# Two of sixteen row maxima as 512-element passes beside a positive difference on ScalarE, and the maxima turned by VectorE instead of TensorE

## What is computed

```python
y = einsum('bsi,oi->bso', x, sign(weight / s)) * (s * scale_param)   # s: mean |weight| of a row
scores = einsum('bhqd,bhkd->bhqk', q, k) / sqrt(16)
attn = softmax(scores, axis=-1)
out = einsum('bhqk,bhkd->bhqd', attn, v)
...
hidden = silu(x @ gate_w.T) * (x @ up_w.T)
x = x + attention(xn) + hidden @ down_w.T
```

## Time and profile before

| | |
|---|---|
| median of 3 runs | 503.11 us (502.55 to 505.74) |
| profiled execution | 502.01 us, of which the span is 500.3 us |
| PE busy | 482.1 us |
| DVE busy | 416.9 us |
| ACT busy | 348.3 us |
| POOL busy | 94.6 us |
| mean granted PE clock | 0.996 |

### The profile page before, as it was taken

How to read it: one execution, slowest core, us unless ns; L and a number is a source line. 1 busy time by engine, 2 the same in 40 slices (tenths; PEclk the granted TensorE clock), 3 DMA queues, 4 the chain that set the end, 5 groups by cost and what they waited for, 6 DMA issues and landing times.

```text
span 500.3 us, 10322 instructions
## 1 busy us (share of the span) xinstructions
PE 482.1 (96%) x4186; PEld 163.9 (33%) x4186; DVE 416.9 (83%) x487; ACT 348.3 (70%) x655; POOL 94.6 (19%) x138
## 2 busy tenths in 40 slices
PE   1899999999998999999999999999999999999996
PEld 1564444433332222222222222222222233333442
DVE  7879869676777999999999999999999955224986
ACT  1943643352338999999999999999999978874000
POOL 4212244434323000000000000000000113241021
PEclk9999999999998999999999999999999999999999
DMA  8843673732103702102102211211120124452321
GB/s 269 273 95 98 163 151 42 200 74 25 20 1 54 135 24 64 41 24 64 41 24 65 41 36 50 42 57 29 42 63 24 35 78 112 105 148 80 104 84 43
DMA packets 31302, 39.02 MB, mean 78 GB/s; under 512 B 6608, under 2 KB 20816, under 8 KB 31256
## 3 DMA queue, kind: packets, MB, share of 16 engines
q1 hardware_dynamic: 22232, 27.34, 18.9%
q0 software_dynamic: 8304, 10.95, 11.9%
q10 hardware_dynamic: 720, 0.08, 0.1%
HBM read 33.24 MB, written 10.35 MB: 87 GB/s over the span
## 4 chain that ended last, share of the span: by engine, by line
PE 94%; DVE 3%; ACT 1%; DMA 1%; issue 1%; ACTq 0%; SPq 0%; DVEq 0%
PE ps L1319 28%; PE ps L1135 19%; PE ps L1250 15%; PE ps L1144 10%; PE ps L1211 5%; PE ps L1198 5%; PE ps L1114 4%; PE ps L1353 3%; PE ps L1286 2%; DVE stats L768 1%; ACT room L709 1%; DVE room L790 1%; PE ps L1106 1%; PE ps L1155 1%; DMA hlo<-x 1%
## 5 line engine op out<-in xcount | busy, mean ns | idle before, releaser
L842 DVE TENSOR_REDUCE nmx<-ps 128x1 f32<-128x1024 f32 x248 | 284.1, 1216 | 14.2 <-PE ps L1144 13.9
L709 ACT ACTIVATE room<-ps 128x512 f32<-128x512 f32 x512 | 271.5, 602 | 21.5 <-PE ps L1286 11.0
L1319 PE MATMUL ps<-room,vcur 128*32 128x256 f32 (+1 forms) x1880 | 159.6, 411 | 0.7 <-ACT room L709 0.7
L1144 PE MATMUL ps<-kA,qst 48*128 48x512 f16 x496 | 142.4, 384 | 0.0
L1250 PE MATMUL ps<-qst,kB 50*128 50x512 f16 x432 | 135.6, 385 | 0.6 <-DVE room L941 0.4
L1135 PE MATMUL ps<-room,wf 128*128 128x512 f16 x448 | 100.6, 379 | 0.0
L1319 PEld LDWEIGHTS ps<-room,vcur 128*32 128x32 f32 x1880 | 37.2, 108 | 94.6 <-issue 53.9
L689 ACT ACTIVATE room<-ps,gsc 128x512 f32<-128x512 f32 x28 | 19.3, 688 | 61.8 <-PE ps L1135 61.8
L1135 PEld LDWEIGHTS ps<-room,wf 128*128 128x128 f16 x448 | 42.4, 98 | 55.1 <-issue 7.2
L1250 PEld LDWEIGHTS ps<-qst,kB 50*128 50x128 f16 x432 | 27.7, 93 | 92.6 <-ACT room L709 71.9
L546 POOL TENSOR_TENSOR hlo<-room,hhi 128x512 f16<-128x512 f32 x28 | 34.0, 1216 | 87.2 <-ACT hhi L619 87.2
(11 more groups left out here) (136 smaller groups left out, 319.4 us busy)
## 6 DMA issues: line engine op xcount, KB each, us to landing
qst<-q_scratch SPq DMA_DIRECT2D x32, 192.0 KB, 3.6
o_scratch<-osb SPq DMA_DIRECT2D x16, 256.0 KB, 2.3
q_scratch<-parts SPq DMA_DIRECT2D x12, 256.0 KB
hlo<-x SPq DMA_DIRECT2D x8, 256.0 KB, 4.6
parts<-x POOLq DMA_DIRECT2D x8, 256.0 KB, 3.9
wf<-gate POOLq DMA_DIRECT2D x14, 128.0 KB, 3.8
wf<-up POOLq DMA_DIRECT2D x14, 128.0 KB, 5.9
wd<-down POOLq DMA_DIRECT2D x1, 1792.0 KB, 13.5
```

Of the source, the lines that this page charges most:

```text
L709: nc.scalar.activation(probs[:, s % 2, r, :], ps[:, bank_of(gp, s, i), :], ACT.Exp, scale=gam_reg[par][r]).then_inc(scores_free, 1)
L842: nc.vector.tensor_reduce(nmx[:, hf, idx:idx + 1], bank_pair(idx % 2), AX.X, ALU.max, negate=True).then_inc(rows_free, 1)
L1144: return nc.tensor.matmul(ps[:, 2 * (idx % 2) + b, :], qst[low:low + KROWS, par, hf, head, qt * P:(qt + 1) * P], kA[low:low + KROWS, par, ...
L1319: mm = nc.tensor.matmul(ps[32 * r:32 * r + 32, values_bank(step_ // TT), of], vcur[:, par, key_tile(r, j), :], probs[:, s % 2, r, of], sta ...
```

## The change

**Two units of sixteen take another form.** In the steps with `step % 8` 4 and 6 before `LATE` (`PAIRED`, `paired`; 26 steps in all) the first of the step's two units is a pair. Its PE matmul on bank 0 uses, instead of the keys of the first half, half the *difference* of the keys of the two halves (`kD`), so that bank 0 holds half of a - b, where a and b are the scores of a query with key n and key n + 512; bank 1 holds b as before. ACT computes `excess` = Relu(2 x bank 0) into SBUF, between its first and second exponential of that step. DVE then makes one pass over 512 elements, bank 1 plus `excess` (that is max(a, b)), with the minimum of the negated sum as its result (`row_max_paired`). The pass waits for ACT's `excess_ready`. The number of PE's matmuls stays.

**The differences.** POOL forms them once from the projected keys in four 128x512 operations (`difference`), among its feed-forward work; SP stores them to `d_scratch` and loads 48 x 512 of them for each group. The evacuation of the values projection on DVE waits for the first of the four.

**The turn of the maxima.** POOL now scales and splits the 128 x 16 table itself, in three 128x16 operations (`split_max`), DVE transposes it in blocks of 32 x 32 (`turn_max`, one 128x32 instruction between the two units of a block's second step), and SP stores it with eight transfers of 2 x 16 x 32 elements instead of four of 16 x 128. PE's transpose, its bank of the ring, and ACT's `take_max` are gone.

```diff
+    PAIRED = [4, 6]
+
+    def paired(step):
+        return step < LATE and step % TT in PAIRED
...
-        if j == T_STEP:
-            taken.append(("t", block_ + 1))
-        elif j == T_STEP + 1:
-            freed.append(("t", block_ + 1))
...
+            def load_differences(g, par):
+                sp.dma_start(kD[0:KROWS, par, :],
+                             d_scratch[bass.ds(g, 1)].rearrange("g t d n -> (g t d) n")).then_inc(kD_loaded[par], 16)
+
             def load_shift(v, par, hf):
                 sp.wait_ge(shift_ready, v + 1)
-                for low in (0, HI):
-                    for part in range(2):
-                        row = low + KROWS + part
-                        dst = qst[row:row + 1, par, hf].rearrange("p h n -> p (h n)")
-                        sp.dma_start(dst, shp[:, hf, part, :]).then_inc(shift_loaded[par][hf], 16)
+                for row in (KROWS, HI + KROWS):
+                    dst = qst[row:row + 2, par, hf].rearrange("p h (t b n) -> p (h t) b n", b=P // SQ, n=SQ)
+                    for b in range(P // SQ):
+                        sp.dma_start(dst[:, :, b, :], shp[b * SQ:(b + 1) * SQ, hf, :]).then_inc(shift_loaded[par][hf], 16)
...
             def split_max(v, hf):
 
-                pool.wait_ge(max_taken, v + 1)
-                nc.gpsimd.tensor_tensor(shp[:, hf, 0, :], mxs[:, :], ones[0:UNITS, :], ALU.mult).then_inc(shift_step, 1)
-                pool.wait_ge(shift_step, v + 1)
-                nc.gpsimd.tensor_tensor(shp[:, hf, 1, :], mxs[:, :], shp[:, hf, 0, :], ALU.subtract).then_inc(shift_ready, 1)
-
+                pool.wait_ge(rows_free, 2 + (v + 1) * UNITS)
+                pool.wait_ge(shift_ready, v)
+                nc.gpsimd.tensor_tensor(mxs[:, :], nmx[:, hf, :], unlift[:, :], ALU.mult).then_inc(split_step, 1)
+                nc.gpsimd.tensor_tensor(mxp[:, 0:UNITS], nmx[:, hf, :], unlift[:, :], ALU.mult).then_inc(split_step, 1)
+                pool.wait_ge(split_step, 2 * (v + 1))
+                nc.gpsimd.tensor_tensor(mxp[:, UNITS:2 * UNITS], mxs[:, :], mxp[:, 0:UNITS],
+                                        ALU.subtract).then_inc(split_ready, 1)
+
+            def difference(stage):
+
+                if stage == 0:
+                    pool.wait_ge(sign_ready, 3)
+                    pool.wait_ge(guarded, 2)
+                    nc.gpsimd.tensor_tensor(diff, y[:, 0, 0:HALF], y[:, 0, HALF:T], ALU.subtract).then_inc(diff_step, 1)
+                elif stage == 1:
+                    pool.wait_ge(diff_step, 1)
+                    pool.wait_ge(out_factors_ready, 1)
+                    nc.gpsimd.tensor_scalar(diff, diff, k_down[:, 0:1], 0.5, ALU.mult, ALU.mult).then_inc(diff_step, 1)
+                elif stage == 2:
+                    pool.wait_ge(diff_step, 2)
+                    nc.gpsimd.tensor_copy(diff_parts[:, 0, :], diff).then_inc(diff_step, 1)
+                else:
+                    pool.wait_ge(diff_step, 3)
+                    nc.gpsimd.tensor_tensor(diff_parts[:, 1, :], diff, diff_parts[:, 0, :],
+                                            ALU.subtract).then_inc(diff_ready, 1)
...
-                if j == t_step(step // TT) + 1 and not (last and s >= STEPS + TT):
-                    block_ = gp * 4 + s // TT
-                    take_max(block_ + 1, LATE_T if step >= LATE else ring_bank["t", block_ + 1])
                 act.wait_ge(probs_free, step + 1)
...
+                    if i == 0 and paired(step):
+                        act.wait_ge(excess_due, pairs_before(step) + 1)
+                        before = [p for p in range(step) if paired(p)]
+                        if before:
+                            act.wait_ge(rows_free, 2 + 2 * UNITS + 2 * before[-1] + 1)
+                        nc.scalar.activation(excess, ps[:, 0, :], ACT.Relu, scale=2.0).then_inc(excess_ready, 1)
...
+            def turn_max(v, hf):
+
+                dve.wait_ge(split_ready, v + 1)
+                nc.vector.transpose(shp[:, hf, :], mxp[:, :]).then_inc(shift_ready, 1)
+
+            def row_max_paired(n, hf, idx, pairs):
+
+                dve.wait_ge(rows_ready, n + 1)
+                dve.wait_ge(excess_ready, pairs + 1)
+                nc.vector.tensor_tensor_reduce(gr[:, 0:HALF], ps[:, 1, :], excess, -1.0, TOP, ALU.add, ALU.min,
+                                               nmx[:, hf, idx:idx + 1]).then_inc(rows_free, 1)
...
-                        mm = half_rows(1 - par, hf, idx, 1 - half)
+                        if i == 0 and paired(step):
+                            assert half == 1
+                            pe.wait_ge(kD_loaded[1 - par], 16 * ((gp_ * 2 + par + 2) // 2))
+                            mm = half_rows(1 - par, hf, idx, 0, kD)
+                            mm.then_inc(excess_due, 1)
+                        else:
+                            mm = half_rows(1 - par, hf, idx, 1 - half)
...
-                if j == T_STEP:
-                    ring_free(("t", block_ + 1))
-                    transpose_max(block_ + 1, 1 - hf, ring_bank["t", block_ + 1])
```

99 lines of the change are left out of this document (57 added, 42 removed), and 2 rows, old and new, of the table dve_order.

## The result

The changed kernel takes 511.63 us (median of 6 runs, 510.25 to 514.26), the kernel before in the same runs 502.89: a ratio of 1.0169, 95% interval 1.0133 to 1.0205. It is slower by 8.7 us, inside the range of 502 to 514, and 3.5 us above the forecast. The profiled execution of it took 512.35 us, with a span of 510.6.

The account below looks back on a forecast made before the run. PE was taken to bound the attention loop, with DVE 0.1 us from it; +5.7 us in the loop, -0.3 for the half block and -0.4 outside gave +5.0 on 503.1, 508.1 us, range 502 to 514.

Parts of the forecast that it names:

- TensorE's floor of 1.11 and 17.76 a block: Attention loop: PE's half step never takes less than 1.11 us, so a block's sixteen halves take 17.76.
- relief rival: Attention loop: PE runs at its floor, 17.91 us a block, 0.30 less than before; 498.7 us in all; chance 0.12.
- Taking the transpose off PE alone would bring nothing: Attention loop: without the pairs, a block would still end at DVE's 18.10 us plus the new turn.
- The fourth exponential's delay, 0.33 a paired step: Paired steps: ACT's fifth operation makes PE's values matmuls start 0.33 us later, 0.66 a block.
- The whole block, 18.65: Attention loop: 17.76 + 0.09 + 0.06 + 0.66 + 0.08 us a block, against 18.21 before, +0.44.
- DVE's block becomes ... 17.4, no longer the bound in sum: Attention loop: fourteen full reductions, two paired units and the turn take DVE 17.4 us a block.
- VectorE's paired unit, 0.81 to free banks and 0.74 to the next start: Paired steps: DVE's pass and read-out take 0.81 us from start to free banks, 0.74 to DVE's next start.
- costly-pass rival: Paired steps: DVE's paired unit costs a full reduction's 1.22 us, total 521; anything above 511 has chance 0.15.
- 1.4 us behind the block's last unit; DVE comes to the turn three units (3.4 us) later. No wait.: DVE's turn in the loop: GpSimd's split is done 1.4 us behind the last unit, before DVE needs it; cost 0.
- At the end of the loop GpSimd may answer late ... Cost 0: Loop's end: a late GpSimd costs 0, as DVE has idle time and PE needs nothing from it for four steps.
- The transposes outside the loop (-0.4) and the half block (-0.3): One transpose before and one behind the loop save 0.2 us each; the final half block loses its transpose, -0.3.
- SP's queue, the keys' difference: Eight shift transfers issue in 4.8 us, hidden by 7 us; GpSimd's four difference operations cost 0 to 0.5, taken as 0.

Follow-up runs that it names:

- ScalarE's part alone: Changed kernel without pairs, but ScalarE still does an unread fifth 512-element operation in steps 4 and 6 of each block: 18.57 us a block.
- the difference first: Changed kernel with ScalarE's positive difference ahead of the first exponential in a paired step, not behind it: 18.62 us a block.
- Moving the call: Changed kernel with GpSimd's first split put ahead of its last hidden low part and the last down-weight transfer: 508.84 us, 1.0102 of the kernel before.
- both splits early: Changed kernel with the first split moved earlier and the last put between GpSimd's store of the second tile's reciprocals and its wait: 508.84 us, 1.0123.
- 256 elements: Changed kernel with ScalarE's difference over 256 of 512 elements in all paired steps but the first: 18.21 us a block.

## Why the prediction was right, and where not

The forecast of +5.0 us was +8.7. The sign and the size in the loop were right, with one cause of two seen there; one step in the sum was wrong that carries most of the rest, the split in the first block.

- **TensorE's floor of 1.11 and 17.76 a block**: right. No half is shorter in any run. Even the relief rival's 17.91 was met by the run whose difference is computed once (17.89).
- **"Taking the transpose off PE alone would bring nothing"**: right, 18.19 against 18.21.
- **The fourth exponential's delay, 0.33 a paired step**: right. The two halves are 0.30 and 0.35 too long, and ScalarE's part alone gives 2 x 0.34 over the floor. The slack in front of TensorE came out as 0.14 us (0.48 less 0.34) and not 0.09. The Trainium skill (ScalarE: Activation LUTs, Step-by-step: what each stage is for) has one element per cycle, 0.833 ns; the trace agrees (0.48 less 0.07 us for 496 elements more is 0.83 ns), but an operation adds about 0.05 to that in the queue.
- **The whole block, 18.65**: measured 18.63. That the two agree so well is in part luck, and hides a difference in the reasons. I took ScalarE's delay plus 0.08 for a bank wait; the runs show two rounds of about the same length: TensorE behind ScalarE (18.57 with ScalarE's part alone, 18.62 with the difference first) and VectorE (18.57, if both its waits were the 0.70 that they are with one pair and with four; the second is 0.76, since TensorE is late there). Which of the two sets the last 0.06 us can't be told. "DVE's block becomes ... 17.4, no longer the bound in sum" led astray: it left out that the pass waits 0.70 us for its operand, more than the 0.51 it saves. It also had 0.05 us from the end of the difference to the pass, which is 0.14. The idle time of "some 1 us a block" was forecast (1.30 measured), but not that nothing is idle between, so that it lengthens VectorE's round.
- **VectorE's paired unit, 0.81 to free banks and 0.74 to the next start**: 0.62 + 0.08 = 0.70 and 0.62. The costly-pass rival is out.
- **"1.4 us behind the block's last unit; DVE comes to the turn three units (3.4 us) later. No wait."**: this step failed, in the first block alone. The sum took a place in the steady loop and applied it to thirteen blocks, of which the first begins while GpSimd still has the feed-forward part's last low part and the down weights in its queue. VectorE waited 2.52 us at its turn there. That costs 20.29 - 18.33 = 2.0 us at full clock, and 1.4 more in the changed kernel's profile, where the clock fell behind it. Moving the call took the ratio from 1.0169 to 1.0102, 3.4 us.
- **"At the end of the loop GpSimd may answer late ... Cost 0"**: VectorE waited 3.18 us for the answer, and the last block is 1.2 us longer in the profile. Whether by this wait isn't shown: with the wait taken down to 0.81 the block was 0.5 shorter with pairs and 0.6 longer without.
- **The transposes outside the loop (-0.4) and the half block (-0.3)**: not seen. The feed-forward part is 0.10 us shorter than in the first profile of the kernel before and 0.09 longer than in the second, the late intervals are 20.38 against 20.41, and 22.04 in both. For the half block the chain has the reason: from 396.1 to 409.3 us, the end of the steady loop and the half block, it is a pass and reductions of VectorE without a break in the changed kernel, and TensorE and ScalarE in the kernel before. So VectorE's reductions, which the change left as they are there, left TensorE nothing to gain.
- **SP's queue, the keys' difference**: no cost was seen. The eight shift transfers take 5.16 us to issue and nothing waits for them in the loop.

```profile
273.29 5.16 SPq L421 DMA_DIRECT2D qst<-shp  x8
```

The sum from the profiles, over the second profile of the kernel before, whose own first block had no fall of the clock: 4.9 for the twelve blocks, 0.4 + 2.0 + 1.4 for the first, 1.2 for the last, 0.1 before the loop, 10.0 with the fractions rounded. With the median of runs it is 8.7: a profile is one execution, and the clock's 1.4 us need not be in all of them. The later start (1.8 us after the first profile, 0.5 after the second) belongs to neither. Of the forecast's terms, the loop's +5.7 came out as 5.3, and the 0.7 us of relief outside did not come.

What stays open is the last block. It is 22.94 in both profiles of the kernel before and 23.3 to 24.4 in every changed one, with or without pairs. In the changed kernel the rows of the chain there are transfers, the store of an output among them at 8.56 us, where it was 6.4 and 6.7; GpSimd issues the residual's loads 0.3 us ahead of the copy that the store follows, in the kernel before 2.1 and 1.7 us ahead. That these loads then run into the store is argued from the order alone; the run with both splits early (1.0 us ahead, 23.63) fits it, the one that also has no pairs (0.8 ahead, 23.84), the one with no pairs alone (0.7 ahead, 23.27) and the one with four pairs (1.6 ahead, 24.06) don't fall in line. It wasn't tried by itself. None of the versions that compute the whole layer beats the kernel before.

## What to carry to other kernels

Work moved from one engine to a second and a third is paid where each hand-over waits: here a pass 0.51 us shorter on VectorE waited 0.70 us for its operand from ScalarE, so with one pair and with four it made the relieved engine's own round longer. Before moving work, look for the engine's slack at the place, not in its sum: ScalarE was 70% busy, but a fifth operation in one step had 0.14 us of it. And when an in-order engine gets a new duty in a loop, read the first and the last round by themselves, with what else stands in its queue there; the steady block says nothing about them.

## What I had not expected of the hardware

**The clock fell behind a short stall, in some executions.** Windows of the first block (six, then four us, then the rest; each row has the us, then busy us and count of PE, PEld, DVE, ACT and POOL, the granted clock, the DMA share and GB/s), the changed kernel and the run with the difference first:

```profile
156.35:162.35 6.00, 4.53 (x46) 1.31 (x48) 3.48 (x5) 4.52 (x9) 3.19 (x6) 1.00 0.37 50
162.35:166.35 4.00, 4.00 (x28) 0.70 (x27) 3.36 (x3) 2.21 (x5) 0.00 (x0) 0.57 1.21 193
166.35:178.06 11.71, 11.68 (x124) 3.09 (x120) 9.67 (x12) 11.26 (x23) 0.62 (x3) 1.00 0.58 107
```

```profile
155.91:161.91 6.00, 4.53 (x46) 1.31 (x48) 3.49 (x5) 4.52 (x9) 3.19 (x6) 1.00 0.43 51
161.91:165.91 4.00, 4.00 (x40) 1.00 (x39) 3.83 (x4) 3.50 (x8) 0.00 (x0) 1.00 1.19 185
```

The same six us with the same 4.53 us of matmuls, and then in one run a granted clock of 0.57, most of it at the lower level (1.2 GHz), with 28 matmuls in 4 us, in the other 1.00 and 40. Of nine profiles with the late first split, eight had a stretch at the lower level in the first block; of three with the early split none; of two of the kernel before one. They aren't all the stall's. In six it began 5.3 to 6.5 us behind the loop's first values matmul, that is behind TensorE's 1.47 us of idle time, which end at 4.8. In the other two (no pairs, 256 elements), and in the kernel before, it began within 0.5 us of the loop's first values matmul, ahead of the stall; in the 4 us before that matmul TensorE was busy 2.7 us, in all fourteen profiles alike, those without a fall too. So the stall that costs 2.0 us by itself cost 3.4 in the changed kernel's profile, and one profile of a kernel doesn't tell which it will be.

**A pass with one operand in PSUM and a running minimum** took 692 ns for 512 elements with 83 ns for its read-out, against 1212 for 1024 elements in a reduction. The first is 1.35 ns an element and the second 1.18, so the second operand doesn't halve the rate here; no run has a reduction of 512 to compare more closely. A pass with both operands in SBUF was not run. **GpSimd's operations** on 128x16 took 0.22 us, where the earlier trace rows have 0.50 for 16x128: fewer elements in a partition are cheaper, though there are as many in all.
